# Rotary embedding in a decoder kernel: halves exchanged by transfers between partitions in place of a second projection, sine product on GpSimd

## The chip, the cores and the metric

The kernel runs on one core of a Trainium2 chip. The metric is the device time of one launch in microseconds (us). The matmul engine is TensorE (PE in the rows, with PEld for its weight loads), VectorE is DVE, ScalarE is ACT, GpSimd is POOL and SyncE, from whose queue the transfers are issued, is SP. All arithmetic is in float32.

## What is computed

A two-layer decoder over 8 batches of 512 rows of width 256. Each layer is self-attention, cross-attention and a feed-forward part, each added to its input and layer-normed. The change touches the self-attention of the second layer alone:

```python
q = einsum('bsd,qd->bsq', x, wq)            # 16 heads of 64
kv_latent = einsum('bsd,ld->bsl', x, w_kv_down)
k = einsum('bsl,ql->bsq', kv_latent, w_k_up)
v = einsum('bsl,ql->bsq', kv_latent, w_v_up)
q = q * cos + rotate_half(q) * sin          # rotate_half(x) = concat(-x[32:], x[:32]) in each head
k = k * cos + rotate_half(k) * sin
scores = q k^T / 8, causal; softmax; times v; times wo^T
```

## The kernel before

`decoder` runs its stages one after another: `attention("a0")`, a cross-attention, a butterfly FFN, `attention("a1")`, `attention("x1")` and a mixture of experts. Stage "a1" is the one in question. It handles 8 batches; a batch has G = 4 groups of 4 heads, a group has 4 tiles of 128 query rows, so a batch has 16 steps. Step s (0 to 15) is group s // 4, tile s % 4, and causality lets tile t see (t+1) x 128 keys.

The work is software-pipelined over steps. In step s PE forms the scores of tile s (`score_head`, L640), transposes the probabilities of tile s-3 (`transpose_head`, L668) and multiplies those of tile s-4 with the values (`times_values`, L689), ACT copies the transposed probabilities out of PSUM (L805) and takes the exponentials of tile s-1 (L810), DVE masks and maximises the scores (L993) and normalises tile s-2 (L1015). Each engine has its own instruction stream in the fixed order head j = 0, 1, 2, 3, then what is left at j = 4. Two heads' scores (j = 0, 1 and j = 2, 3) are made together.

`tasks` (L250) puts the rest between the heads. For the next group four *items* are made: for each of its two pairs of heads a q item (i even) and a k item (i odd). Items 0 and 1 stand in the group's first step, at j = 1 and j = 3, items 2 and 3 in its second. For the last group of a batch, the items belong to the next batch and stand one step later (steps 13 and 14), since step 12 holds the transposition of the next x ("xT") and the latent ("lat"). The values ("v", L596) come in the steps after, and the output projection of the previous batch ("y", L608), 16 matmuls each, stands at j = 1 of steps 4 to 7. A group's first scores wait until all low parts of its items are there (L622).

An item goes over four engines:

- PE (L537 to L547): the projection with the plain weights into one PSUM bank, then the one with weights whose halves of 32 columns are exchanged in each head (`wqs`, `wupk[:, 1]`) into the next. A q item has two contraction tiles, a k item one; the trace shows two matmul records for each.
- DVE (L939): plain times cos into `rsum[i % 2]`, exchanged times sin into `rsin`.
- POOL (L883): `rsum += rsin`; then (L887, L890) the low part, `rsum` less its high part.
- ACT (L751, L753): the high part. It doesn't stand at the item's own place but at the very end of the step (L824 to L827), item by item, and each waits for its `rot_sum`.

POOL's stream of an item is: wait for `rot_done`, add, wait for `hi` (the ACT copy), subtract. DVE starts an item only when the low part of the item two before it is there (L932). There are four PSUM banks `A` for scores and projections, taken in turn, and two, `T`, for the transposes: head j + 2 can be transposed when ACT has copied head j.

SP issues the stage's loads (L478, L480) and once per batch the next x tile (L486); otherwise it is idle here.

Of the kernel before, what the change touches and what calls it, by code (L numbers as in the profile page):

```python
# [212 lines left out]
def attention(nc, sh, kind, w):  # L213
# [68 lines left out]
    def work_jobs(work):  # L282
        if work[0] == "xT":
            return [(("xT", dt), "xt") for dt in range(DT)]
        if work[0] == "lat":
            return [("lat", "act")]
        if work[0] == "v":
            return [(work, "dve" if a0 else "v")]
        if work[0] == "y":
            return [(work, "dve")]  # L290
        if a1:
            return [((*work, 0), "dve"), ((*work, 1), "rot")]
        if x1:
            return [(work, "ql")]
        return [(work, ("dve", "kl")[work[2]])]
# [26 lines left out]
    with ExitStack() as ctx:  # L322
# [48 lines left out]
        if a1:  # L371
            wqs = sb("wqs", [P, DT, IN])
            lat = sb("lat", [P, S])
            wdn = sb("wdn", [P, DT, P])
            wupk = sb("wupk", [P, 2, IN])
            wupv = sb("wupv", [P, IN])
            cos = sb("cos", [P, S])
            sin = sb("sin", [P, S])
            rsum = sb("rsum", [P, 2, S])
            rsin = sb("rsin", [P, S])  # L380
# [41 lines left out]
        chain = sem("chain")  # L422
        sems = {"full": a_full, "act": a_act, "dve": a_dve, "xt": xt_done, "v": v_done,
# [43 lines left out]
        if a1:  # L467
            loads += [(wq[:], tiled(w["w_q"])), (wqs[:], tiled(w["w_q_swapped"])), (wdn[:], tiled(w["w_down"])),
                      (wupk[:, 0, :], w["w_up_k"]), (wupk[:, 1, :], w["w_up_k_swapped"]),
                      (wupv[:], w["w_up_v"]), (table[:], w["causal"]), (cos[:], w["cos"]), (sin[:], w["sin"])]  # L470
# [5 lines left out]
        @block.sync  # L476
        def _(sp):
            sp.dma_start(xin[:], sh.x_all[:, 0:QT, :]).then_inc(xin_in, 16)  # L478
            for to, src in loads:
                sp.dma_start(to, src).then_inc(weights, 16)  # L480
            if x1:
                sp.dma_start(ctxT[:], tiled(w["ctxT"][0])).then_inc(ctx_in, 16)
            with sp.Fori(1, B) as b:

                sp.wait_ge(xt_done, b * DT)
                sp.dma_start(xin[:], sh.x_all[:, bass.ds(b * QT, QT), :]).then_inc(xin_in, 16)  # L486
                if x1:

                    sp.wait_ge(v_done, b * N_V)
                    sp.dma_start(ctxT[:], w["ctxT"][bass.ds(b, 1)].rearrange("a (t p) n -> p (a t) n", p=P))\  # L490
                      .then_inc(ctx_in, 16)

        @block.tensor
        def _(pe):
# [13 lines left out]
            def project(seg, turn, b, work):  # L508
# [22 lines left out]
                if a1:  # L531
# [5 lines left out]
                    for sw in range(2):  # L537
                        name = (*work, sw)
                        pe.wait_ge(*seg.empty(turn, name))
                        bank = A[seg.bank(name)]  # L540
                        if i % 2 == 0:
                            for t in range(DT):
                                mm = pe.matmul(bank[:], (wq, wqs)[sw][:, t, col], xT[:, t, :],
                                               start=(t == 0), stop=(t == DT - 1))
                        else:
                            mm = pe.matmul(bank[:], wupk[:, sw, col], lat[:], start=True, stop=True)
                        mm.then_inc(a_full, 1)  # L547
# [189 lines left out]
        def _(act):  # L737
# [30 lines left out]

            def project(seg, turn, b, work):
# [18 lines left out]
            def step(seg, turn, b, s, prev, own, nxt):  # L788
# [8 lines left out]
                for j in range(5):  # L797
# [15 lines left out]
                    for at, work in found:  # L813
                        if at == j and not (a1 and work[0] == "item"):
                            project(seg, turn, b + (work in NEXT and s >= U - QT), work)
# [13 lines left out]
            def begin():  # L829
                for work in START:  # L830
                    project(start, 0, 0, work)
# [8 lines left out]
        def _(pool):  # L840
# [33 lines left out]
            if a1:  # L874
                pool.sem_inc(rot_sum, 2)
                pool.sem_inc(low, LOW_GROUP)
                pool.wait_ge(ready, N_READY)
                with pool.Fori(0, B) as b:
                    for g in range(G):
                        for i in range(4):  # L880
                            gp = g % 2
                            pool.wait_ge(rot_done, b * 4 * G + (4 * g + i + 1))
# [11 lines left out]
        def _(dve):  # L894
# [18 lines left out]
            def low_parts(seg, turn, b, g, i):  # L913
# [16 lines left out]
                elif a1:  # L930

                    dve.wait_ge(low, b * LOW_GROUP * G + (LOW_GROUP * g + (LOW_ITEM[i + 2] if i < 2 else LOW_GROUP + LOW_ITEM[i - 2])))  # L932
                    for sw in range(2):
                        name = ("item", g, i, sw)
                        if sw:

                            dve.wait_ge(rot_sum, b * 4 * G + (4 * g + i + 2))
                        dve.wait_ge(*seg.full(turn, name))
                        nc.vector.tensor_tensor((rsum[:, i % 2, :], rsin[:])[sw], A[seg.bank(name)][:], (cos, sin)[sw][:],  # L939
                                                ALU.mult).then_inc((a_dve, rot_done)[sw], 1)  # L940
# [1148 lines left out]
def combine(nc, sh, place, gates, results, out):  # L2089

    with ExitStack() as ctx:  # L2091
# [58 lines left out]
        "a1_w_q", "a1_w_q_swapped", "a1_w_down", "a1_w_up_k", "a1_w_up_k_swapped", "a1_w_up_v", "a1_w_o",  # L2150
# [44 lines left out]
def laid_out(a):  # L2195
# [6 lines left out]
    def swapped(wt):  # L2202

        n = wt.shape[0]
        return wt.reshape(n, -1, 2, 32)[:, :, ::-1].reshape(n, -1)

# [21 lines left out]
    def placed_high(wt, side):  # L2228

        out = np.zeros((HIGH, FT, P, 2), np.float32)  # L2230
        for h in range(HIGH):
# [19 lines left out]
            "a1_w_q": wq1, "a1_w_q_swapped": swapped(wq1), "a1_w_down": a["L1_attn_w_kv_down"].T,  # L2251
            "a1_w_up_k": wku1, "a1_w_up_k_swapped": swapped(wku1), "a1_w_up_v": a["L1_attn_w_v_up"].T,
# [24 lines left out]
```

## Time and profile before

| | us |
|---|---|
| median of 3 runs (lowest, highest) | 4617.55 (4616.95, 4618.64) |
| the profiled execution: its own time | 4615.9 |
| its span, first to last instruction | 4614.1 |
| PE, DVE, ACT, POOL busy in the span | 3915.6, 2717.7, 2094.8, 1178.2 |
| mean granted TensorE clock | 0.932 |

The page's list by line gives busy time and what ended the idle time before. Matmuls are pipelined, so the pace of a run of matmuls is read from the start of one group of records to the start of the next, not from one record's length. Times of a timeline are from the start of the span. Stage "a1" lies between 1562 us (its first load) and 2779 us.

### The profile page before, as it was taken

To read this page: it belongs to the slowest core of one execution; us is meant where nothing else is said; L and a number is where in the kernel's file an instruction comes from. 1 tells how busy PE (TensorE), PEld (TensorE's weight loads), DVE (VectorE), ACT (ScalarE), POOL (GpSimd) and SP (SyncE) were. 2 spreads that over 40 slices of the span, in tenths; PEclk is the share of its full clock that TensorE was granted. 3 is DMA by queue.
4 is the path that set the end of the run, shared out by engine and by line. 5 is a ranking of instruction groups with operands and counts; after the bars stand their busy time and mean duration, and the time that the engine had idled before them with its cause. 6 is when DMAs were issued, how large, how long until landed. Compare 5 with 4: busy or idle time off the path is not lost. (4 is left out here: it accounts for less than half of the span.)

```text
span 4614.1 us, 81513 instructions
## 1 busy us (share of the span) xinstructions
PE 3915.6 (85%) x25804; PEld 2614.9 (57%) x25805; DVE 2717.7 (59%) x7518; ACT 2094.8 (45%) x4994; POOL 1178.2 (26%) x980
## 2 busy tenths in 40 slices
PE   6999999996869799999999997999999526999980
PEld 3555555565768555555555565666666414666650
DVE  5888888886867466666665654566656421111116
ACT  4777776772342165455545553555555201111110
POOL 2444444443400132232222211122111251000004
PEclk9999999997789899999999998999999758999995
DMA  2000000001020100000000001000000521000003
GB/s 64 6 6 6 6 6 6 1 1 46 14 85 1 59 6 6 1 6 6 6 1 6 1 1 44 7 6 5 5 6 1 172 105 47 30 30 30 30 30 106
DMA packets 80047, 115.62 MB, mean 25 GB/s; under 512 B 14369, under 2 KB 66017, under 8 KB 78945
## 3 DMA queue, kind: packets, MB, share of 16 engines
q1 hardware_dynamic: 73568, 94.56, 6.1%
q0 software_dynamic: 6144, 16.79, 1.2%
q8 instruction: 187, 3.06, 0.3%
q14 instruction: 148, 1.20, 0.1%
HBM read 63.09 MB, written 31.46 MB: 20 GB/s over the span
## 5 line engine op out<-in xcount | busy, mean ns | idle before, releaser
L805 ACT ACTIVATE a_pT<-a_T 128x512 f32<-128x512 f32 (+3 forms) x1024 | 526.0, 514 | 469.8 <-PE a_T L668 460.2
L810 ACT ACTIVATE a_t<-a_t,a_neg 128x512 f32<-128x512 f32 (+3 forms) x1024 | 650.7, 635 | 97.8 <-DVE a_neg L1007 97.4
L668 PE MATMUL a_T<-ident,a_t 128*128 128x128 f32 x3328 | 554.1, 283 | 6.5 <-ACT a_pT L805 6.2
L1015 DVE TENSOR_SCALAR a_t<-a_t,a_inv 128x512 f32<-128x512 f32 (+3 forms) x768 | 528.0, 688 | 9.0
L668 PEld LDWEIGHTS a_T<-ident,a_t 128*128 128x128 f32 x3328 | 396.6, 142 | 171.1 <-issue 68.4
L629 PE MATMUL a_A<-a_kpad,a_qs 128*128 128x512 f32 x1024 | 393.5, 467 | 72.0 <-DVE a_mx L993 50.8
L883 POOL TENSOR_TENSOR a_rsum<-a_rsum,a_rsin 128x512 f32<-128x512 f32 x128 | 162.7, 1271 | 978.0 <-DVE a_rsin L939 976.9
L854 POOL TENSOR_TENSOR a_t<-a_t,a_inv 128x512 f32<-128x512 f32 x256 | 284.2, 1132 | 477.3 <-DVE a_inv L1011 477.3
L993 DVE CUSTOM_DVE_ANT_0 a_t<-a_A,a_decay 128x512 f32<-128x512 f32 x512 | 343.9, 683 | 85.9 <-PE a_A L629 62.2
L993 DVE CUSTOM_DVE_ANT_0 a_t<-a_A,a_table 128x384 f32<-128x384 f32 (+3 forms) x512 | 247.2, 483 | 171.1 <-PE a_A L640 166.9
L854 POOL TENSOR_TENSOR x_t<-x_t,x_inv 128x576 f32<-128x576 f32 x128 | 158.1, 1257 | 725.0 <-DVE x_inv L1011 725.0
L2072 DVE COPY experts_y<-experts_Y 128x256 f32<-128x256 f32 x72 | 30.6, 425 | 514.0 <-PE experts_Y L2010 514.0
L2022 PE MATMUL experts_H<-ex_w,experts_xgT 128*128 x576 | 268.2, 609 | 47.6 <-ACT experts_xgT L2049 47.6
L629 PEld LDWEIGHTS a_A<-a_kpad,a_qs 128*128 128x128 f32 x1024 | 161.7, 193 | 210.1 <-issue 108.7
L805 ACT ACTIVATE x_pT<-x_T 128x512 f32<-128x512 f32 (+1 forms) x320 | 189.3, 592 | 177.8 <-PE x_T L668 135.7
L2010 PE MATMUL experts_Y<-ex_w,experts_hT 128*128 x1152 | 260.5, 379 | 1.0 <-DVE experts_hT L2081 1.0
L2010 PEld LDWEIGHTS experts_Y<-ex_w,experts_hT 128*128 128x128 f32 x1152 | 218.8, 190 | 61.3 <-issue 35.2
L2113 POOL DMA_INDIRECT combine_got<-moe_results,moe_place x64 | 60.9, 951 | 691.5 <-PEq L2091 658.0
L993 DVE CUSTOM_DVE_ANT_0 x_t<-x_A,x_table 128x512 f32<-128x512 f32 x256 | 170.9, 685 | 107.2 <-PE x_A L640 105.1
L689 PE MATMUL a_O<-a_pT,a_v 128*64 128x128 f32 x2560 | 210.9, 286 | 25.0 <-ACT a_oT L822 23.7
L685 PE MATMUL a_O<-a_pT,a_v 128*32 128x128 f32 x4096 | 221.5, 290 | 3.9 <-ACT a_pT L805 3.9
L640 PE MATMUL a_A<-a_khl,a_qhl 64*128 64x128 f32 (+3 forms) x1536 | 188.0, 350 | 38.5 <-issue 15.4
(275 smaller groups left out, 7387.8 us busy)
## 6 DMA issues: line engine op xcount, KB each, us to landing
ex_w<-in_f_w_dram SPq DMA_DIRECT2D x16, 1024.0 KB, 13.6
moe_sent<-route_zeros SPq DMA_DIRECT2D x1, 9216.0 KB, 29.6
experts_xg<-moe_sent SPq DMA_DIRECT2D x72, 128.0 KB, 2.0
moe_results<-experts_y SPq DMA_DIRECT2D x72, 128.0 KB, 1.7
a_xin<-x_all SPq DMA_DIRECT2D x16, 512.0 KB, 2.9
x_xin<-x_all SPq DMA_DIRECT2D x16, 512.0 KB, 2.9
x_all<-in_x_dram SPq DMA_DIRECT2D x1, 4096.0 KB, 14.5
out_dram<-x_all SPq DMA_DIRECT2D x8, 512.0 KB
```

The source lines that it names most:

```text
L629: mm = pe.matmul(A[seg.bank(name)][:, 0:keys(u)], qs[:, gp, q], kpad[:, gp, hl, j, 0:keys(u)], start=(n == 0), stop=(n == 1))
L640: mm = pe.matmul(A[seg.bank(at)][:, 0:keys(u)], q_hl[r, gp, ql, j // 2, q], k_hl[r, gp, kl_, j // 2, 0:keys(u)], start=(n == 0), stop=(n = ...
L668: mm = pe.transpose(bank[:, kt, :], t_of(u, j, kt * P, (kt + 1) * P), sh.ident[:])
L685: mm = pe.matmul(O[hh][32 * j:32 * j + 32, q], v_sb[:, kt, 8 * hh + 2 * j + par, :], p_tile(u, j, kt), start=(par == 0 and qt == 0 and kt ...
L689: mm = pe.matmul(O[pr][64 * half:64 * half + 64, q], v_sb[:, kt, col], p_tile(u, j, kt), start=(kt == 0), stop=last, skip_group_check=True)
L805: nc.scalar.activation(to, of, ACT.Copy).then_inc(t_empty, 1)
L810: nc.scalar.activation(t_of(u_e % U, j, 0, n), t_of(u_e % U, j, 0, n), ACT.Exp, bias=neg[:, slot, j:j + 1], scale=SCALE, accum_out=total[: ...
L854: nc.gpsimd.tensor_tensor(t_of(u_n % U, j, 0, NK), t_of(u_n % U, j, 0, NK), inv[:, u_n % 4, j:j + 1].to_broadcast([P, NK]), ALU.mult).then ...
L993: nc.vector.tensor_tensor_reduce(t_of(s, j, 0, n), A[seg.bank(name)][:, 0:n], table[:, at:at + n], 1.0, LOWEST, ALU.mult if a0 else ALU.ad ...
L1015: nc.vector.tensor_scalar(t_of(u_n % U, j, 0, m), t_of(u_n % U, j, 0, m), inv[:, u_n % 4, j:j + 1], None, ALU.mult).then_inc(normed, 1)
L2010: mm = pe.matmul(Y[parity][:], hT[:, f, :], w2[:, bass.ds(e, 1), f, :].rearrange("p a d -> p (a d)"), start=(f == 0), stop=(f == FT - 1))
L2022: mm = pe.matmul(H[half][:], xgT[:, dt, :], w1[:, bass.ds(e, 1), dt, half * 512:(half + 1) * 512] .rearrange("p a f -> p (a f)"), start=(d ...
```

## The change

The exchanged projections and their weights go. ACT copies each item's raw projection from PSUM to `raw` (four buffers) at the item's own place in the step; SP issues four transfers, each of 32 partitions x 2 KB, that write it to `raw_swapped` (two buffers) with neighbouring blocks of 32 partitions exchanged; POOL multiplies that with sin into `rsin` and then adds and subtracts as before. DVE keeps the cos product. Its wait for the raw copy is new, and the bank is now counted free by the cos product. The high part stays on ACT at the end of the step.

```diff
-            return [((*work, 0), "dve"), ((*work, 1), "rot")]
+            return [(work, "rot")]
...
-            wqs = sb("wqs", [P, DT, IN])
-            wupk = sb("wupk", [P, 2, IN])
+            wupk = sb("wupk", [P, IN])
+            raw = sb("raw", [P, 4, S])
+            raw_swapped = sb("rawswapped", [P, 2, S])
...
+            def swap_halves(b, n):
+
+                wait_apart(sp, (weights, 16 * len(loads)), (raw_done, b * 4 * G + n + 1), (sin_done, b * 4 * G + n + 3))
+                for k in range(4):
+                    sp.dma_start(raw_swapped[32 * k:32 * k + 32, n % 2, :],
+                                 raw[32 * (k ^ 1):32 * (k ^ 1) + 32, n % 4, :]).then_inc(swapped[n % 2], 16)
+
+            if a1:
+                with sp.Fori(0, B - 1) as b:
+                    for n in range(4 * G):
+                        swap_halves(b, n)
+                        if n == 3:
+                            sp.wait_ge(xt_done, b * DT + DT)
+                            sp.dma_start(xin[:], sh.x_all[:, bass.ds(b * QT + QT, QT), :]).then_inc(xin_in, 16)
...
-                    for sw in range(2):
-                        name = (*work, sw)
-                        pe.wait_ge(*seg.empty(turn, name))
-                        bank = A[seg.bank(name)]
...
+                    pe.wait_ge(*seg.empty(turn, work))
+                    bank = A[seg.bank(work)]
+                    if i % 2 == 0:
+                        for t in range(DT):
+                            mm = pe.matmul(bank[:], wq[:, t, col], xT[:, t, :], start=(t == 0), stop=(t == DT - 1))
+                    else:
+                        mm = pe.matmul(bank[:], wupk[:, col], lat[:], start=True, stop=True)
+                    mm.then_inc(a_full, 1)
...
+            def raw_copy(seg, turn, b, work):
+                _, g, i = work
+                n = 4 * g + i
+                act.wait_ge(*seg.full(turn, work))
+                act.wait_ge(sin_done, b * 4 * G + n + 1)
+                nc.scalar.activation(raw[:, n % 4, :], A[seg.bank(work)][:], ACT.Copy).then_inc(raw_done, 1)
...
-                        if at == j and not (a1 and work[0] == "item"):
-                            project(seg, turn, b + (work in NEXT and s >= U - QT), work)
+                        if at == j:
+                            (raw_copy if a1 and work[0] == "item" else project)(
+                                seg, turn, b + (work in NEXT and s >= U - QT), work)
...
                 for work in START:
+                    if a1 and work[0] == "item":
+                        raw_copy(start, 0, 0, work)
                     project(start, 0, 0, work)
...
+                pool.sem_inc(sin_done, 4)
...
-                            pool.wait_ge(rot_done, b * 4 * G + (4 * g + i + 1))
+                            n = 4 * g + i
+                            pool.wait_ge(swapped[n % 2], b * 32 * 4 * G + 64 * (n // 2 + 1))
+                            nc.gpsimd.tensor_tensor(rsin[:], raw_swapped[:, n % 2, :], sin[:],
+                                                    ALU.mult).then_inc(sin_done, 1)
+                            pool.wait_ge(sin_done, b * 4 * G + (n + 5))
+                            pool.wait_ge(rot_done, b * 4 * G + (n + 1))
                             nc.gpsimd.tensor_tensor(rsum[:, i % 2, :], rsum[:, i % 2, :], rsin[:],
                                                     ALU.add).then_inc(rot_sum, 1)
                             pool.wait_ge(hi, b * HI_GROUP * G + (HI_GROUP * g + HI_ITEM[i]))
...
-                    for sw in range(2):
-                        name = ("item", g, i, sw)
-                        if sw:
-
-                            dve.wait_ge(rot_sum, b * 4 * G + (4 * g + i + 2))
-                        dve.wait_ge(*seg.full(turn, name))
-                        nc.vector.tensor_tensor((rsum[:, i % 2, :], rsin[:])[sw], A[seg.bank(name)][:], (cos, sin)[sw][:],
-                                                ALU.mult).then_inc((a_dve, rot_done)[sw], 1)
+                    name = ("item", g, i)
+                    dve.wait_ge(*seg.full(turn, name))
+                    dve.wait_ge(raw_done, b * 4 * G + (4 * g + i + 1))
+                    nc.vector.tensor_tensor(rsum[:, i % 2, :], A[seg.bank(name)][:], cos[:], ALU.mult)\
+                      .then_inc(rot_done, 1)
```

## Rows read from the trace of the kernel before

**Rows 1.** Busy time by stretch: us, busy (instructions) of each engine, PEclk, DMA, GB/s.

```profile
1724.00:2620.00 896.00, 839.64 (x5268) 508.17 (x5266) 560.86 (x1704) 468.20 (x1365) 246.92 (x192) 0.99 0.01 4
```

**Rows 2.** Timeline of PE, first scores of groups 0 to 3, step 13, next batch.

```profile
2023.22 0.55 PE L640 MATMUL a_A<-a_khl,a_qhl 64*128 64x128 f32 x6 [2.98 <-issue]
...
2055.21 0.55 PE L640 MATMUL a_A<-a_khl,a_qhl 64*128 64x128 f32 x6
...
2100.46 0.55 PE L640 MATMUL a_A<-a_khl,a_qhl 64*128 64x128 f32 x6
...
2134.25 0.55 PE L640 MATMUL a_A<-a_khl,a_qhl 64*128 64x128 f32 x6
...
2142.20 0.62 PE L640 MATMUL a_A<-a_khl,a_qhl 64*128 64x256 f32 x6
...
2172.62 0.55 PE L640 MATMUL a_A<-a_khl,a_qhl 64*128 64x128 f32 x6 [2.92 <-issue]
```

**Rows 3.** Timeline of PE: step 1's items of group 0, and where step 3 begins.

```profile
2037.39 1.88 PE L543 MATMUL a_A<-a_xT,a_wqs 128*128 128x512 f32 x4
2039.20 0.62 PE L640 MATMUL a_A<-a_khl,a_qhl 64*128 64x256 f32 x6
...
2040.47 1.88 PE L546 MATMUL a_A<-a_lat,a_wupk 128*128 128x512 f32 x4
2042.28 0.79 PE L640 MATMUL a_A<-a_khl,a_qhl 64*128 64x384 f32 x6
...
2048.97 0.96 PE L640 MATMUL a_A<-a_khl,a_qhl 64*128 64x512 f32 x6
```

**Rows 4.** Timeline of ACT at the turn of steps 0 and 1.

```profile
2036.25 0.63 ACT L753 ACTIVATE a_khl<-a_rsum 128x512 fp32r<-128x512 f32 x1 [2.61 <-POOL a_rsum L883]
2036.79 0.47 ACT L805 ACTIVATE a_pT<-a_T 128x384 f32<-128x384 f32 x1
...
2037.54 0.48 ACT L805 ACTIVATE a_pT<-a_T 128x384 f32<-128x384 f32 x1
```

**Rows 5.** Timeline of POOL, and one operation of DVE, over the same steps.

```profile
2034.94 1.27 POOL L883 TENSOR_TENSOR a_rsum<-a_rsum,a_rsin 128x512 f32<-128x512 f32 x1
2036.96 1.41 POOL L890 TENSOR_TENSOR a_khl<-a_rsum,a_khl 128x512 fp32r<-128x512 f32 x1 [0.74 <-ACT a_khl L753]
...
2031.02 1.45 DVE L1015 TENSOR_SCALAR a_t<-a_t,a_inv 128x384 f32<-128x384 f32 x1
```

**Rows 6.** Transfers: issues with KB each and us to landing; one line's issue ns.

```profile
a_xin<-x_all SPq DMA_DIRECT2D x16, 512.0 KB, 2.9
x_ctxT<-in_ctxT_dram SPq DMA_DIRECT2D x8, 64.0 KB, 1.9
moe_results<-experts_y SPq DMA_DIRECT2D x72, 128.0 KB, 1.7
L490 SPq DMA_DIRECT2D x_ctxT<-in_ctxT_dram x7: 376/381/406, 2847.3 to 3452.7; - x7
```

**Rows 7.** Timeline of PE: the last batch's first item, and an output projection.

```profile
2619.50 0.55 PE L640 MATMUL a_A<-a_khl,a_qhl 64*128 64x128 f32 x6
...
2622.19 1.88 PE L543 MATMUL a_A<-a_xT,a_wq 128*128 128x512 f32 x4
...
1758.84 3.62 PE L608 MATMUL a_A<-a_wo,a_oT 128*128 128x256 f32 x16
```

**Rows 8.** Busy time by stretch after PE's idle time at a batch's end.

```profile
2024.00:2027.60 3.60, 3.60 (x15) 1.96 (x14) 1.26 (x7) 2.17 (x6) 0.00 (x0) 0.55 0.02 5
2028.00:2029.00 1.00, 1.00 (x4) 0.43 (x3) 0.51 (x1) 0.00 (x0) 0.00 (x0) 1.00 0.00 0
```

**Rows 9.** Timeline of the stage's start: PE's first work, second projection, first scores.

```profile
1580.49 1.94 PE L517 MATMUL a_A<-ident,a_xin 128*128 128x128 f32 x8 [26.38 <-DVEq L911]
...
1588.80 1.88 PE L543 MATMUL a_A<-a_xT,a_wqs 128*128 128x512 f32 x4
...
1604.58 0.90 PE L640 MATMUL a_A<-a_khl,a_qhl 64*128 64x128 f32 x6 [5.31 <-POOL a_khl L890]
```

More of the change, by code:

```diff
@@ L422, in attention @@
         chain = sem("chain")
+        raw_done = env.sem("raw_done") if a1 else None
+        swapped = [env.sem(f"swapped{i}") for i in range(2)] if a1 else None
+        sin_done = env.sem("sin_done") if a1 else None
         sems = {"full": a_full, "act": a_act, "dve": a_dve, "xt": xt_done, "v": v_done,
@@ L467, in attention @@
         if a1:
-            loads += [(wq[:], tiled(w["w_q"])), (wqs[:], tiled(w["w_q_swapped"])), (wdn[:], tiled(w["w_down"])),
-                      (wupk[:, 0, :], w["w_up_k"]), (wupk[:, 1, :], w["w_up_k_swapped"]),
+            loads += [(wq[:], tiled(w["w_q"])), (wdn[:], tiled(w["w_down"])),
+                      (wupk[:], w["w_up_k"]),
                       (wupv[:], w["w_up_v"]), (table[:], w["causal"]), (cos[:], w["cos"]), (sin[:], w["sin"])]
@@ L482, in _ @@
                 sp.dma_start(ctxT[:], tiled(w["ctxT"][0])).then_inc(ctx_in, 16)
+            def swap_halves(b, n):
[10 more added lines that the diff above has]
+                            sp.dma_start(xin[:], sh.x_all[:, bass.ds(b * QT + QT, QT), :]).then_inc(xin_in, 16)
+                for n in range(4 * G):
+                    swap_halves(B - 1, n)
+                return
             with sp.Fori(1, B) as b:
@@ L536, in project @@
                         pe.wait_ge(a_act, b + 1)
-                    for sw in range(2):
-                        name = (*work, sw)
-                        pe.wait_ge(*seg.empty(turn, name))
-                        bank = A[seg.bank(name)]
[L541 to L547, printed above, removed]
+                    pe.wait_ge(*seg.empty(turn, work))
[6 more added lines that the diff above has]
+                    mm.then_inc(a_full, 1)
                     return
@@ L2149 @@
         "f0_w_exp_b", "f0_low", "f0_high", "f0_up_bias", "f0_w_con", "f0_b_con", "f0_down_bias",
-        "a1_w_q", "a1_w_q_swapped", "a1_w_down", "a1_w_up_k", "a1_w_up_k_swapped", "a1_w_up_v", "a1_w_o",
+        "a1_w_q", "a1_w_down", "a1_w_up_k", "a1_w_up_v", "a1_w_o",
         "x1_w_q", "x1_w_k1", "x1_w_v1", "x1_w_k2", "x1_w_v2", "x1_w_o", "x1_b_o",
@@ L2200, in split_pairs @@
         return wt.reshape(n, 2, 4, 2, 16).transpose(0, 1, 3, 2, 4).reshape(n, 4, 64)
-    def swapped(wt):
-        n = wt.shape[0]
-        return wt.reshape(n, -1, 2, 32)[:, :, ::-1].reshape(n, -1)
     def pairs(stage):
@@ L2250, in laid_out @@
             "f0_down_bias": a["L0_ffn_down_bias"].reshape(row),
-            "a1_w_q": wq1, "a1_w_q_swapped": swapped(wq1), "a1_w_down": a["L1_attn_w_kv_down"].T,
-            "a1_w_up_k": wku1, "a1_w_up_k_swapped": swapped(wku1), "a1_w_up_v": a["L1_attn_w_v_up"].T,
+            "a1_w_q": wq1, "a1_w_down": a["L1_attn_w_kv_down"].T,
+            "a1_w_up_k": wku1, "a1_w_up_v": a["L1_attn_w_v_up"].T,
             "a1_w_o": a["L1_attn_wo"].T,
```

## Prediction

> **What bounds the kernel now.** The change lies inside stage "a1", so I read the busy times of that stage by stretch first, then the order of PE's work through one batch, then ACT and POOL beside it, as the change lengthens a chain that runs over these two. In the six steady batches PE is busy for 839.6 of 896 us, at a granted clock of 0.99 of 2.4 GHz, ACT for 468, DVE for 561, POOL for 247 [rows 1]. PE sets the pace; its only long idle time is 3 us at each batch's end. One batch takes 149.4 us: its groups 32.0, 45.2, 33.8 and 38.4 us, the last with 8.0 for step 12 [rows 2]. Group 1 carries four output projections of 3.6 us [rows 7].
>
> The place to look at is the end of a step with items. ACT takes the first item's high part, then idles 2.6 us until the second item's sum is there [rows 4]: POOL subtracts (1.28 us) and adds (1.27 us) in between [rows 5]. That idle time costs PE nothing today, since PE has projections to run meanwhile.
>
> **What goes.** Per q item four matmul records on exchanged weights, 2037.39 to 2039.20 with 0.1 for the next operation: 1.72 us. Per k item two of the four in 2040.47 to 2042.28: 0.86 us [rows 3]. 64 items of each kind: 64 x 2.58 = 165 us, 5.2 us per group, all on the engine that sets the pace. Were nothing else to happen, this would be the gain, 3.6%. DVE loses 128 products, worth nothing by themselves, as it is busy 63% of the stage [rows 1]. Two of the stage's loads go, 1.5 of 5.5 MB; PE starts 18 us after the stage's first load [rows 9], and a quarter of the bytes is 4 us (bounds 0 and 5).
>
> **What comes, priced from R, the end of an item's raw copy on ACT.** SP wakes (0.1 us, the gap ACT to POOL in [rows 4, 5]), issues four transfers of 64 KB; an issue is 0.38 us, so I take 0.4 from one to the next and the fourth starts 1.3 us after R; landing 1.9 us after issue [rows 6]. Landed at R + 3.3. No row shows a 32-partition transfer inside SBUF: the nearest are 64 KB (1.9), 128 KB (1.7) and, inside SBUF but 512 KB, 2.9. I take the one of equal size; bounds for the landing R + 2.7 and R + 4.6. Then POOL's product, an operation of the add's form, 1.27 + 0.05, the add 1.27 + 0.05, ACT's high part with wake 0.7: R + 6.6. POOL's subtraction, 1.35: R + 7.95. Only now comes the second item's product in POOL's stream, 1.25, its add, 1.3, and ACT's second high part, 0.7: **ACT is free at R + 11.2 us**. The second item's transfers are hidden behind the first's, its POOL work isn't.
>
> The raw copies are on ACT, priced like the high part's, 0.6 us [rows 4], 128 x 0.6 = 77 us; they lie partly in time in which ACT waits. SP's 512 issues block nothing but the next x tile, which is needed ten steps later. One more POOL operation per item also collides with DVE: a normalisation took 1.45 us beside POOL's add [rows 5]. DVE's slack covers that; if all of an operation's 1.27 us were waited for, without cover, it would be 163 us in all.
>
> What queues behind ACT's two waits: its copies of transposed probabilities. PE can go on through the next step's first scores, heads 0 and 1, and an item, up to the transpose of head 2, which needs a T bank that only ACT empties. The slack there is 5.0 us after the last item of the step (scores 0.55, two transposes and two value products 2.1, item 1.8, scores 0.55, [rows 3]). R is 1.2 us before that last item's end (scores and two transposes 1.0, the k item 0.9, less the 0.7 of the copy), so PE stands from about R + 6.2 until R + 11.8. DVE's new wait for the raw copy comes through the same ACT stall; as the cos product is all that hangs on it, and POOL needs that only after its own product, I cost it at nothing; if that cover went, it would be up to 0.7 us in a step.
>
> **The cycle of a group** (F: ACT free).
> - First scores to R of item 0: 2.7 to the projection's start, 1.8 projection, 0.6 copy: 5.1 [rows 7]; 5.8 at a batch's start, with the low clock there.
> - R to the R of item 2: 11.2 to F, two heads' copy and exponential at 0.75, copy 0.6: 13.3. In group 3, where the exponentials are 256 keys wide in place of 128, I estimate 0.95 for a head: 13.7.
> - R of item 2 to F: 11.2.
> - F to the next group: transpose 0.55 later, then 0.5, value product 0.6, transpose 0.5, values 1.0, 3.3 with the waits, and step 3 from [rows 3, 2]: 2048.97 to 2055.21, 6.2. Sum 9.5. In group 3 it is step 15's rest, 4.1 with two value blocks, and 3.0 idle at the loop's end: 7.1.
> - Clock: after the 3 us idle at a batch's end the granted clock was 0.55 for 3.6 us, the lower of its two levels for nearly all of it [rows 8], so 1.6 us of work are lost. The second stall's aftermath is such a place; the first one's lies under the second. 1.6 per group.
>
> So group 0: 5.8 + 13.3 + 11.2 + 9.5 + 1.6 = 41.4 (was 32.0). Group 2: 40.7 (was 33.8). Group 1: two of its four output projections (step 5's and 6's) fall into stalls, two don't: 40.7 + 7.2 = 47.9 (was 45.2). Group 3: 8.0 + 5.1 + 13.7 + 11.2 + 7.1 + 1.6 = 46.7 (was 38.4). A batch grows by 9.4 + 6.9 + 2.7 + 8.3 = 27.3 us, six of them 164. The last batch has no items in group 3: 19. The first has no output projections: I take 10 for group 0, whose before is shortest, and 24 for the others: 34. At the start the four items go strictly one after another, 6.6 + 0.6 each, from R at 1589.5 (the first projection ends where the exchanged one begins, 1588.8, and the copy takes 0.7): low parts at 1619 in place of 1604.6 [rows 9]: 14. Loads -4. **Sum: +227 us.** On the profiled execution's 4615.9 us that is 4843; the median of the runs lies 1.7 us above it, so 4845, 4.9% slower.
>
> A rule that would make it another way: the Trainium skill, "DMA: Bandwidth & Descriptors", Rules for kernel authors, says to issue a transfer early, compute, and wait late, so that its fixed cost overlaps. By it the sum would be -165 - 4; the order of POOL's stream, with the product first and ACT waiting for it in the same step, is why I don't take it.
>
> **Rivals.**
> 1. *The chain is covered* (faster). If PE isn't held at the transpose of head 2 because the two waits on ACT end within its slack, R + 6.2, only the removal counts: 4617.6 - 169 = 4449 us. For it: today's 2.6 us of ACT idle costs nothing, ACT is idle for 48% of the stage [rows 1]. Against: POOL's five operations and two ACT copies alone, with no transfer at all, are 7.9 us after R. It decides from a chain of R + 6.2 us down; even a landing at once leaves it longer. Between, each us off the chain is worth some 66 us (two chains per group, 62, and the start's four). Break-even needs 3.4 us off, a landing with R. Chance 0.05.
> 2. *The clock stays low* (much slower). With two idle spells per 20 us, PE could stay at 1.2 GHz through the 14.6 us between F and the next R, which is PE's own time: up to 13 us more for 31 groups, 5250 us. Against: after that idle time the clock is full again four microseconds later [rows 8]. Chance 0.05.
> 3. *Less slack lost than counted*: ACT makes up for its stall faster, and the output projections and norm steps hide more of it; half of the added time, 4730 us. For it: group 2's own 1.8 us over group 0 today are waits that a stalled ACT would hide. Chance 0.10.
> 4. That the exchanged matmuls stay is excluded by the diff; no chance.
>
> **The numbers.** The forecast has 0.80. Bounds within it: the chain's landing from 2.7 to 4.6 makes -40 and +86; the clock term 0 to twice its size -50 and +50; they rarely add up. Range 4725 to 4945, so that it takes in rival 3. About 0.2% (9 us) is what a measurement of this kernel can tell from no change: faster by more 0.06, within 0.01, slower by more 0.93.
>
> **What would show it.** Right: ACT idle before L751 as well as before L753, about 3.5 and 4 us each time, ended by POOL's add; POOL idle before its product, ended by a transfer or the raw copy; PE idle before L668, ended by ACT's copy L805, some 5 us twice per group; PE busy in the stage 165 us less plus what the clock costs; groups of 41, 48, 41 and 47 us. Wrong: PE's wait for L805 stays under 1 us (rival 1), a mean granted clock near 0.5 in the stage (rival 2), or landings far from 1.9 us. If the transfers were late beyond R + 4.6, POOL's idle time before the product would exceed 3 us of each pair and the sum would be too small.

## The result, and the profile after

The changed kernel takes 4908.9 us (median of four runs, 4905.6 to 4919.4) against 4617.6 for the kernel before in the same comparison: a ratio of **1.063**, 95% interval 1.0616 to 1.0653. That is +291 us; forecast were +227 and 4845, with a range up to 4945. The profiled execution took 4911.5 us, its span is 4909.6.

First the page of the kernel after: its head, three groups of its part 5 (busy us, mean ns of one | idle us of the engine just before them and what ended it) and one line of part 6 (KB each, us from issue to landing).

```profile
span 4909.6 us, 81900 instructions
PE 3877.1 (79%) x25420; PEld 2615.2 (53%) x25421; DVE 2647.1 (54%) x7390; ACT 2168.4 (44%) x5122; POOL 1337.5 (27%) x1108
L686 PE MATMUL a_T<-ident,a_t 128*128 128x128 f32 x3328 | 599.3, 300 | 321.6 <-ACT a_pT L830 321.3
L913 POOL TENSOR_TENSOR a_rsin<-a_rawswapped,a_sin 128x512 f32<-128x512 f32 x128 | 162.8, 1272 | 1122.3 <-DMA a_rawswapped<-a_raw 1122.3
L970 DVE TENSOR_TENSOR a_rsum<-a_A,a_cos 128x512 f32<-128x512 f32 x128 | 88.6, 692 | 371.6 <-ACT a_raw L792 370.5
a_rawswapped<-a_raw SPq DMA_DIRECT2D x512, 64.0 KB, 2.0
```

PE now idles 321.6 us before its transposes, for ACT's copy that empties the T bank. In the kernel before, the same group stands with 6.5 us. Yet PE's busy time fell by 38.5 us only (3915.6 before), though the removed matmuls are worth 165. The stage alone says why; first the kernel before, then the kernel after, each from the stage's first load to the next stage's, to within 0.3 us (busy times of PE, PEld, DVE, ACT, POOL, then the granted clock). The kernel before ends this stage at 2786 us, not at 2779: its last layer norm runs until 2785.7.

```profile
1562.00:2786.00 1224.00, 1118.91 (x7008) 677.97 (x7008) 743.37 (x2272) 624.21 (x1817) 328.63 (x256) 0.98 0.03 9
```

```profile
1567.45:3075.14 1507.69, 1075.24 (x6624) 675.43 (x6624) 672.97 (x2145) 698.44 (x1945) 488.29 (x384) 0.85 0.11 29
2006.00:2008.00 2.00, 2.00 (x14) 1.34 (x13) 0.00 (x0) 1.72 (x6) 0.15 (x1) 0.50 0.03 8
```

The stage grew by 284 us. PE's busy time there fell by 44, so, if the removed records were worth the forecast's 165 us, those that stayed are 165 - 44 = 121 us longer, at a clock of 0.85 in place of 0.98. PE's idle time grew from 105 to 432 us, by 327. And -165 + 121 + 327 is these 284 us, but for rounding. The lower row is a stretch just after a stall: PE works all the time, at 0.50, the lower of its two levels.

The third view is the timeline of PE, at the first scores of batch 0, of batch 1, and of one later batch's four groups and the next batch (start us, length us).

```profile
1624.16 0.69 PE L658 MATMUL a_A<-a_khl,a_qhl 64*128 64x128 f32 x4 [21.23 <-POOL a_khl L924]
1792.22 0.55 PE L658 MATMUL a_A<-a_khl,a_qhl 64*128 64x128 f32 x6
...
1973.25 0.44 PE L658 MATMUL a_A<-a_khl,a_qhl 64*128 64x128 f32 x4 [0.32 <-issue]
2016.09 0.44 PE L658 MATMUL a_A<-a_khl,a_qhl 64*128 64x128 f32 x4
2066.66 0.44 PE L658 MATMUL a_A<-a_khl,a_qhl 64*128 64x128 f32 x4
2108.72 0.44 PE L658 MATMUL a_A<-a_khl,a_qhl 64*128 64x128 f32 x4
2155.62 0.54 PE L658 MATMUL a_A<-a_khl,a_qhl 64*128 64x128 f32 x5 [1.31 <-ACT a_v L809]
...
2883.75 0.55 PE L658 MATMUL a_A<-a_khl,a_qhl 64*128 64x128 f32 x6
```

The groups take 42.8, 50.6, 42.1 and 46.9 us (forecast 41.4, 47.9, 40.7, 46.7; [rows 2] has before). Batch 0 takes 168.1 us, the six steady ones 1091.5, or 181.9 each where 149.4 were [rows 1, 2].

Last the chain itself, in the timeline of all engines in group 3 of that batch; the answer to [rows 4, 5].

```profile
2121.50 0.60 ACT L792 ACTIVATE a_raw<-a_A 128x512 f32<-128x512 f32 x1 [1.74 <-PE a_A L562]
2122.18 5.03 SPq L491 DMA_DIRECT2D a_rawswapped<-a_raw  x8
...
2126.11 1.27 POOL L913 TENSOR_TENSOR a_rsin<-a_rawswapped,a_sin 128x512 f32<-128x512 f32 x1 [26.89 <-DMA a_rawswapped<-a_raw]
2127.54 1.26 POOL L917 TENSOR_TENSOR a_rsum<-a_rsum,a_rsin 128x512 f32<-128x512 f32 x1 [0.16 <-POOL a_rsin L913]
2128.83 0.63 ACT L769 ACTIVATE a_qhl<-a_rsum 128x512 fp32r<-128x512 f32 x1 [4.30 <-POOL a_rsum L917]
...
2130.76 1.26 POOL L913 TENSOR_TENSOR a_rsin<-a_rawswapped,a_sin 128x512 f32<-128x512 f32 x1
...
2133.47 0.63 ACT L771 ACTIVATE a_khl<-a_rsum 128x512 fp32r<-128x512 f32 x1 [4.01 <-POOL a_rsum L917]
2134.01 0.58 ACT L830 ACTIVATE a_pT<-a_T 128x512 f32<-128x512 f32 x1
2134.73 1.08 PE L686 MATMUL a_T<-ident,a_t 128*128 128x128 f32 x4 [5.46 <-ACT a_pT L830]
```

R, the end of the raw copy, is 2122.10. POOL's product starts at R + 4.0, the second high part ends at R + 12.0, and 0.6 us later PE starts the transpose for which it has waited 5.46 us.

### The profile page after: what moved, and what is told of

It reads as the page before. It is cut to its first block and busy times, and to the rows that moved or that the text cites. A ratio compares the mean times of both kernels' runs of the same rounds, so it can differ in the third digit from the quotient of the medians.

```text
span 4909.6 us, 81900 instructions
## 1 busy us (share of the span) xinstructions
PE 3877.1 (79%) x25420; PEld 2615.2 (53%) x25421; DVE 2647.1 (54%) x7390; ACT 2168.4 (44%) x5122; POOL 1337.5 (27%) x1108
## 5 line engine op out<-in xcount | busy, mean ns | idle before, releaser
L686 PE MATMUL a_T<-ident,a_t 128*128 128x128 f32 x3328 | 599.3, 300 | 321.6 <-ACT a_pT L830 321.3
L686 PEld LDWEIGHTS a_T<-ident,a_t 128*128 128x128 f32 x3328 | 423.4, 151 | 508.7 <-issue 400.0
L913 POOL TENSOR_TENSOR a_rsin<-a_rawswapped,a_sin 128x512 f32<-128x512 f32 x128 | 162.8, 1272 | 1122.3 <-DMA a_rawswapped<-a_raw 1122.3
L647 PE MATMUL a_A<-a_kpad,a_qs 128*128 128x512 f32 x1024 | 394.7, 469 | 72.3 <-DVE a_mx L1024 47.7
L970 DVE TENSOR_TENSOR a_rsum<-a_A,a_cos 128x512 f32<-128x512 f32 x128 | 88.6, 692 | 371.6 <-ACT a_raw L792 370.5
L707 PE MATMUL a_O<-a_pT,a_v 128*64 128x128 f32 x2560 | 229.8, 304 | 31.5 <-ACT a_oT L848 25.8
L658 PE MATMUL a_A<-a_khl,a_qhl 64*128 64x128 f32 (+3 forms) x1536 | 205.1, 376 | 50.2 <-POOL a_khl L924 21.2
L658 PEld LDWEIGHTS a_A<-a_khl,a_qhl 64*128 64x128 f32 x1536 | 126.4, 203 | 213.5 <-issue 112.4
```

Source lines behind the costliest of these rows:

```text
L647: mm = pe.matmul(A[seg.bank(name)][:, 0:keys(u)], qs[:, gp, q], kpad[:, gp, hl, j, 0:keys(u)], start=(n == 0), stop=(n == 1))
L658: mm = pe.matmul(A[seg.bank(at)][:, 0:keys(u)], q_hl[r, gp, ql, j // 2, q], k_hl[r, gp, kl_, j // 2, 0:keys(u)], start=(n == 0), stop=(n = ...
L686: mm = pe.transpose(bank[:, kt, :], t_of(u, j, kt * P, (kt + 1) * P), sh.ident[:])
L707: mm = pe.matmul(O[pr][64 * half:64 * half + 64, q], v_sb[:, kt, col], p_tile(u, j, kt), start=(kt == 0), stop=last, skip_group_check=True)
L913: nc.gpsimd.tensor_tensor(rsin[:], raw_swapped[:, n % 2, :], sin[:], ALU.mult).then_inc(sin_done, 1)
```

## The experiments

**Theory A** is the forecast's: each pair of items is a serial chain over ACT, SP, the transfer and POOL; its two waits stand in ACT's fixed order ahead of the copies that empty the T banks, so PE stands. The price is 66 us of time per us of chain. **Theory B**: the time is the extra product on GpSimd itself, its collisions with DVE and the lower clock; the wait is a symptom. Ratios are to the kernel before on the same chip, with their 95% intervals.

### The chain shortened and lengthened

*No transfer.* POOL reads the raw copy directly, and SP's transfers go: the kernel leaves out the exchange of halves.

```diff
-                            pool.wait_ge(swapped[n % 2], ...)
-                            nc.gpsimd.tensor_tensor(rsin[:], raw_swapped[:, n % 2, :], sin[:],
+                            pool.wait_ge(raw_done, b * 4 * G + (n + 1))
+                            nc.gpsimd.tensor_tensor(rsin[:], raw[:, n % 4, :], sin[:],
```

> Edit: SP issues no exchange; POOL multiplies the raw copy itself with sin, so the rotation takes the wrong halves (the exchange is left out). Theory A (the chain from an item's raw copy R to ACT's release sets PE's pace; two such chains per group with items, 62, and four items at the start, so 66 us of time per us of chain): POOL starts 0.1 us after R in place of 4.0, the chain falls from 12.0 to 8.1 us, 3.9 x 66 = 257 us less: 4652 us (4600 to 4700). Theory B (the transfers are covered by the rest of ACT's and POOL's order; the loss is the POOL product and PE's lower clock): at most 60 us less, 4850 or more.

4630.9 us, 1.0065 (1.0048 to 1.0082), within theory A's bounds and far below theory B's 4850. PE's idle time before the transposes is 95 us instead of 322:

```profile
L669 PE MATMUL a_T<-ident,a_t 128*128 128x128 f32 x3328 | 576.2, 291 | 95.1 <-ACT a_pT L813 94.0
```

*Doubled.* Four more transfers per item, into a buffer that nobody reads, ahead of the four that count; POOL waits for all eight.

```diff
-                for k in range(4):
-                    sp.dma_start(raw_swapped[...
+                for k, to in [(k, to) for to in (twin, raw_swapped) for k in range(4)]:
+                    sp.dma_start(to[...
```

> Edit: four more transfers of the same size, to a buffer that nobody reads, issued ahead of the four that count. Theory A: 4 x 0.6 us of issue more on the chain, 2.4 x 66 = 158 us: 5067 us (5030 to 5110), and ACT's wait before L769 2.4 us longer, the one before L771 unchanged. Theory B: below 4950.

5093.9 us, 1.1075 (1.1057 to 1.1094). The chain in its timeline:

```profile
2214.49 0.59 ACT L793 ACTIVATE a_raw<-a_A 128x512 f32<-128x512 f32 x1
...
2217.60 2.49 SPq L492 DMA_DIRECT2D a_rawswapped<-a_raw  x4
...
2221.59 1.26 POOL L914 TENSOR_TENSOR a_rsin<-a_rawswapped,a_sin 128x512 f32<-128x512 f32 x1 [7.60 <-DMA a_rawswapped<-a_raw]
...
2226.82 1.26 POOL L914 TENSOR_TENSOR a_rsin<-a_rawswapped,a_sin 128x512 f32<-128x512 f32 x1 [0.54 <-DMA a_rawswapped<-a_raw]
...
2229.53 0.63 ACT L772 ACTIVATE a_khl<-a_rsum 128x512 fp32r<-128x512 f32 x1 [4.59 <-POOL a_rsum L918]
```

From R (2215.08) to ACT free (2230.16) it is 15.1 us, 3.1 more than after: 2.5 for the first item, and 0.54 because SP's sixteen issues now make the second item's landing late too. The expectation had 2.4 for the first and nothing for the second, so it was short: the time rose by 206 us against the changed kernel (by the ratios, below), where 158 were expected.

*POOL's order.* Both products and sums of a pair first, then both subtractions; `rsin` has two buffers.

```diff
-                        for i in range(4):
...
+                        for pair in range(2):
+                            for i in (2 * pair, 2 * pair + 1):
...
+                                nc.gpsimd.tensor_tensor(rsum[:, i % 2, :], rsum[:, i % 2, :], rsin[:, i % 2, :],
+                                                        ALU.add).then_inc(rot_sum, 1)
+                            for i in (2 * pair, 2 * pair + 1):
...
+                                nc.gpsimd.tensor_tensor(part[:, gp, 1, i // 2, :], rsum[:, i % 2, :],
+                                                        part[:, gp, 0, i // 2, :], ALU.subtract).then_inc(low, 1)
```

> Edit: POOL does product and sum of both items of a step before it waits for the first high part; rsin gets a second buffer. Theory A: the second sum is ready at R + 4.0 + 4 x 1.35 = R + 9.4 in place of R + 11.4, ACT is free at R + 10.1, 1.9 us earlier, in 62 chains (not at the start): 4909 - 118 = 4791 us (4760 to 4830). Theory B, in which POOL's number of operations or its collisions with DVE count: no change, since POOL does the same operations.

4769.7 us, 1.0371 (1.0354 to 1.0389). POOL does the same operations as in the changed kernel, so by theory B nothing should have changed. In its timeline the second product no longer waits behind the first item's subtraction:

```profile
1987.97 0.60 ACT L792 ACTIVATE a_raw<-a_A 128x512 f32<-128x512 f32 x1 [4.09 <-PE a_A L562]
...
1992.54 1.27 POOL L914 TENSOR_TENSOR a_rsin<-a_rawswapped,a_sin 128x512 f32<-128x512 f32 x1 [23.23 <-DMA a_rawswapped<-a_raw]
...
1995.35 1.28 POOL L914 TENSOR_TENSOR a_rsin<-a_rawswapped,a_sin 128x512 f32<-128x512 f32 x1
...
1998.00 0.63 ACT L771 ACTIVATE a_khl<-a_rsum 128x512 fp32r<-128x512 f32 x1 [2.12 <-POOL a_rsum L918]
```

R to ACT free is 10.1 us, 1.9 less than after.

The changed kernel itself, run once more on a second chip, gives the fixed point (4907.4 us, 1.0621, 1.0605 to 1.0638):

> The changed kernel itself, once more, as the yardstick of this chip, on which the kernel before takes 4601 us in place of 4617. Both theories: the same ratio as on record, 1.063 (1.061 to 1.066), 4893 us.

From the mean of its two ratios, 1.0628, the steps are -2.6% of 4601 us for 1.9 us less chain (118 us, 62 per us), +4.5% for 3.1 us more (206 us, 66 per us) and -5.6% for the 3.9 us between R and the start of POOL's product (259 us, 66 per us). The stage alone, from its first load to the next stage's, is free of what chips and runs differ by elsewhere: it takes 1507.7 us in the changed kernel, 1382.5 with POOL's new order, 1710.7 doubled and 1249.0 with no transfer, so 66, 65.5 and 66 us per us. Three points on one line: the slope that the prediction set.

### One part at a time

*The sine product on DVE*, at the end of DVE's step, with the transfers kept.

```diff
+            def sine(b, g, i):
...
+                nc.vector.tensor_tensor(rsin[:], raw_swapped[:, n % 2, :], sin[:], ALU.mult).then_inc(sin_done, 1)
...
-                            nc.gpsimd.tensor_tensor(rsin[:], raw_swapped[:, n % 2, :], sin[:],
-                                                    ALU.mult).then_inc(sin_done, 1)
```

> Edit: the transfers stay, the sine product goes back to DVE, which makes it at the end of the step from the exchanged copy in SBUF. Theory A: the chain loses POOL's two products but for one of DVE's: R + 4.0, product 0.8, sum 1.35, high part 0.7, subtraction 1.35, sum 1.3, high part 0.7: ACT free at R + 10.2 in place of R + 12.0, 1.8 x 66 = 119 us less, ratio to before about 1.037. Theory B (DVE, standing until the second item's transfer has landed, becomes what PE waits for): not below 1.055.

4809.9 us, 1.0414 (1.0399 to 1.0430).

```profile
L992 DVE TENSOR_TENSOR a_rsin<-a_rawswapped,a_sin 128x512 f32<-128x512 f32 x128 | 99.3, 776 | 168.5 <-DMA a_rawswapped<-a_raw 163.9 <-POOL a_rsum L914 4.3
L686 PE MATMUL a_T<-ident,a_t 128*128 128x128 f32 x3328 | 591.7, 297 | 186.3 <-ACT a_pT L830 168.4 <-DVE a_t L1049 17.6
L658 PE MATMUL a_A<-a_khl,a_qhl 64*128 64x128 f32 (+3 forms) x1536 | 201.1, 369 | 93.7 <-DVE a_mx L1027 63.7
```

The product is shorter there (776 ns in place of 1272) and off POOL, which takes 99 us off the change, where 119 were expected. For DVE's order now holds the wait for the transfer, and PE waits for DVE as well: 17.6 us before the transposes, and 63.7 before scores, where the changed kernel has 10.2.

*The second projection back*, read by ACT's raw copy and POOL's product; no transfers. It asks what the copy and the product cost by themselves.

```diff
-            return [(work, "rot")]
+            return [((*work, 0), "rot"), ((*work, 1), "raw")]
...
+                                mm = pe.matmul(bank[:], (wq, wqs)[sw][:, t, col], xT[:, t, :],
...
-                nc.scalar.activation(raw[:, n % 4, :], A[seg.bank(work)][:], ACT.Copy).then_inc(raw_done, 1)
+                nc.scalar.activation(raw[:, n % 4, :], A[seg.bank((*work, 1))][:], ACT.Copy).then_inc(raw_done, 1)
```

> Edit: the transfers are undone and the second projection is back; ACT copies the exchanged projection from PSUM and POOL multiplies that with sin. What is left of the change is the product on GpSimd and ACT's copy. Theory A: the chain is that of the kernel without transfer, R + 8.1, and PE's 165 us come back but fill the holes in which PE stands there (94 us before L668): 4631 + 165 - 94 less some 30 us of low clock = 4672 us, ratio 1.015 (1.005 to 1.025). Theory B (the product's place on GpSimd is the main loss): above 1.04.

4736.7 us, 1.0258 (1.0242 to 1.0274): just above what was expected.

```profile
L673 PE MATMUL a_T<-ident,a_t 128*128 128x128 f32 x3328 | 570.4, 289 | 65.5 <-ACT a_pT L817 64.6
L551 PE MATMUL a_A<-a_lat,a_wupk 128*128 128x512 f32 x256 | 126.6, 617 | 18.5 <-DVE a_rsum L956 15.4 <-ACT a_raw L779 3.1
```

PE's new waits are 59 us for ACT and some 11 for a bank; the mean clock falls from 0.93 to 0.92. So the change can be taken apart: product and copy, with the matmuls kept, +119 us (this run); the matmuls' removal brings -89 of the 165 (from here to the kernel with no transfer, 1.0258 to 1.0065); the transfers add 259. Together +289, as these are steps along one row of ratios. Of the 165 a part is lost again in waits: PE's wait for ACT before the transposes rises from 64.6 to 94.0 us, that for DVE before these scores from 14.4 to 44.8. And the prices hold for this order of steps: with the waits put later (below), the same transfers cost 43 us, not 259.

### The wait put later

*Deferred.* ACT takes the high parts one step later, at j = 2 and 4, so that the chain has a whole step; POOL's order as above, four buffers of `rsum`, and at the stage's start all four raw copies come ahead of the first high part.

```diff
+                late = [(at, work) for at, work in tasks(s - 1, prev, own, nxt) if work[0] == "item"] \
+                    if a1 and own and s > 0 else []
...
+                    for at, work in late:
+                        if at + 1 == j:
+                            project(seg, turn, b + (work in NEXT and s - 1 >= U - QT), work)
...
-                for _, work in found:
-                    if a1 and work[0] == "item":
-                        project(seg, turn, b + (work in NEXT and s >= U - QT), work)
```

> Edit: as pool_order, and ACT takes an item's high part one step later (at j = 2 and j = 4 of the next step), with four rsum buffers, so that ACT and PE don't wait inside the step in which the item was made. Theory A: PE isn't held; the 165 us of exchanged projections are won, less some waits in the batch's last step: 4490 us (4440 to 4560), PE's wait for ACT's copies under 50 us in the stage, clock back at 0.98 or more. Theory B (clock, collisions of POOL with DVE, or ACT's extra copies): above 4750.

4532.8 us, 0.9844 (0.9823 to 0.9865): **faster than both kernels**. Transfers, product on GpSimd and raw copies are all there as in the changed kernel; only the order of POOL's and ACT's streams differs, and some 360 us are gone: 118 with POOL's order (1.0371 above), the rest with the later waits, of which 12.5 at the stage's start (first scores 44.2 us after its first load in place of 56.7). That decides against theory B as the main cause; what it names comes back below, in a smaller size. Placed one head earlier still (j = 1 and 3), it is the same, 4545.6 us on the second chip, 0.9842 (0.9829 to 0.9856):

```diff
-                        if at + 1 == j:
+                        if at == j:
```

> Edit: as deferred, with each high part one head earlier (j = 1 and j = 3 of the next step). Theory A: each batch's end, where PE waited 4.0 us for the last low part and then ran at the low clock, comes 1 to 2 us earlier; against that ACT may wait up to 1 us for the first sum (ready at R + 6.7, when the next step's j = 1 comes). Between 20 us less and 10 us more than deferred: ratio to before 0.980 to 0.987. Theory B, that PE is held by ACT again at this place: above 0.99.

But it is some 55 us short of what theory A expected (4490 us where the kernel before takes 4617, a ratio of 0.972; the removed matmuls alone would be 0.964), and the clock in the stage is 0.93, not back at 0.98. In the stage PE idles 165 us in place of 105, and the records that stayed are some 31 us longer. The list by line of the deferred kernel:

```profile
L686 PE MATMUL a_T<-ident,a_t 128*128 128x128 f32 x3328 | 564.8, 287 | 2.3 <-ACT a_pT L832 1.8
L658 PE MATMUL a_A<-a_khl,a_qhl 64*128 64x128 f32 (+3 forms) x1536 | 196.7, 363 | 107.6 <-POOL a_khl L926 47.7 <-DVE a_mx L1026 46.2 <-ACT a_xT L799 9.9
```

The stall at the transposes is gone, and 94 us stand before scores instead: 47.7 for the last low part before a batch's first scores, 46.2 for a maximum of DVE (5.3 and 7.0 in the kernel before). The latter in its timeline, in group 2:

```profile
2079.32 1.27 POOL L917 TENSOR_TENSOR a_rsin<-a_rawswapped,a_sin 128x512 f32<-128x512 f32 x1 [16.01 <-DMA a_rawswapped<-a_raw]
...
2083.63 1.22 DVE L173 SCALAR_TENSOR_TENSOR a_scratch<-a_scratch 128x4 f32<-128x4 f32 x1
2084.80 1.26 POOL L926 TENSOR_TENSOR a_qhl<-a_rsum,a_qhl 128x512 fp32r<-128x512 f32 x1
2084.96 4.11 DVE L145 TENSOR_SCALAR x_all<-x_all,a_mv,a_scratch  x4
...
2087.29 1.31 POOL L917 TENSOR_TENSOR a_rsin<-a_rawswapped,a_sin 128x512 f32<-128x512 f32 x1
2089.59 0.41 DVE L1026 CUSTOM_DVE_ANT_0 a_t<-a_A,a_table 128x256 f32<-128x256 f32 x1
...
2090.06 1.33 PE L658 MATMUL a_A<-a_khl,a_qhl 64*128 64x384 f32 x6 [6.10 <-DVE a_mx L1026]
```

POOL runs almost without a gap from 2079 to 2089, and beside it DVE's layer norm stretches: four operations of L145 take 4.11 us, the one of L173 on 128 x 4 elements 1.22. At their own lengths (0.41 and 0.16, below) they would be 3.5 us shorter, over half of the 6.10 that PE waits; what the rest is isn't shown. Two more runs ask what belongs to which.

*The kernel before, deferred in the same way*: its second projection stays, no transfers.

```diff
-                            dve.wait_ge(rot_sum, b * 4 * G + (4 * g + i + 2))
+                            dve.wait_ge(rot_sum, b * 4 * G + (4 * g + i + 1))
...
+                    for at, work in late:
+                        if at + 1 == j:
+                            project(seg, turn, b + (work in NEXT and s - 1 >= U - QT), work)
```

> The kernel before, with its second projection and without transfers, but with the reordering of the deferred kernel: ACT's high parts one step later, POOL's two sums of a pair ahead of its two subtractions, four buffers of rsum and two of rsin. It asks how much of the deferred kernel's 0.984 is the reordering and how much the removed matmuls. Theory A (PE's own work sets the pace of before, its ACT idle time of 2.6 us costs nothing): the reordering gives nothing there, 4610 to 4625 us on a chip where before takes 4617, a ratio of 0.998 to 1.005 (the low parts of each batch's last items come some 4 us later, which may cost up to 30 us, 1.006). Rival C (the held ACT already cost something before): 0.985 to 0.995, and then the exchange by transfers would bring little of its own.

4584.2 us, 0.9968 (0.9956 to 0.9981): the reordering brings 0.3% by itself, between theory A's best case (0.998, at the interval's edge) and rival C's least (0.995, outside it), so that the held ACT cost at most a little in the kernel before. So of the deferred kernel's 1.6%, some 1.2% (0.9844 / 0.9968 = 0.988) belong to the exchange by transfers.

*Deferred, no transfer*, edited as in the first experiment:

```diff
-                                nc.gpsimd.tensor_tensor(rsin[:, i % 2, :], raw_swapped[:, n % 2, :], sin[:],
+                                nc.gpsimd.tensor_tensor(rsin[:, i % 2, :], raw[:, n % 4, :], sin[:],
```

> The deferred kernel with no transfers: POOL multiplies the raw projection itself with sin, so the exchange of halves is left out. It asks where the deferred kernel loses the 1.9% that lie between its 0.984 and the 0.965 of the removed matmuls alone. Theory A: the transfers are hidden but for one place, the last low part of each batch's items, for which PE waits 4.0 us eight times; without the landing of 4.0 us that wait goes, with the low clock after it: 30 to 50 us less than the deferred kernel, a ratio to before of 0.973 to 0.978. Rival D (the loss is the collision of DVE and POOL, and ACT's 128 raw copies, all of which stay): within 10 us of the deferred kernel, 0.982 to 0.987.

4484.6 us, 0.9750 (0.9734 to 0.9766), 43 us below the deferred kernel by the ratios. The size is theory A's, the place only in part. For the kernel before deferred, then for the deferred one without transfers, the scores in the list by line:

```profile
L640 PE MATMUL a_A<-a_khl,a_qhl 64*128 64x128 f32 (+3 forms) x1536 | 187.6, 349 | 35.3 <-POOL a_khl L890 21.9 <-ACT a_xT L774 9.9 <-DVE a_mx L993 3.1
```

```profile
L641 PE MATMUL a_A<-a_khl,a_qhl 64*128 64x128 f32 (+3 forms) x1536 | 190.0, 353 | 81.7 <-POOL a_khl L909 37.1 <-DVE a_mx L1009 33.0 <-ACT a_xT L782 9.9
```

The wait for the low part fell only from 47.7 to 37.1, and nearly half of that at the stage's start (15.5 to 10.8); the wait for DVE fell from 46.2 to 33.0, and the kernel's mean clock rose from 0.917 to 0.927. So the expectation named the place wrongly: the 43 us are spread over both waits and the clock after them. The layer norm of the stage, between 1600 and 2750 us, in the kernel before deferred, the deferred one, and the one without transfers (length of one in ns: least, median, most):

```profile
L145 DVE TENSOR_SCALAR x_all<-x_all,a_mv,a_scratch x28: 406/407/414, 1820.0 to 2701.4; - x24, 128x256 f32<-128x256 f32 x4
```

```profile
L145 DVE TENSOR_SCALAR x_all<-x_all,a_mv,a_scratch x32: 400/1345/1382, 1808.7 to 2715.3; - x24, 128x256 f32<-128x256 f32 x8
```

```profile
L145 DVE TENSOR_SCALAR x_all<-x_all,a_mv,a_scratch x32: 399/407/1411, 1797.4 to 2666.5; - x24, 128x256 f32<-128x256 f32 x8
```

The same operation takes 0.41 us, or 1.35 to 1.41 where POOL works beside it; without transfers it meets POOL less often. What stays without transfers comes with the product on GpSimd or with the raw copies on ACT, which no deferred run parts: 33 us of waiting for DVE where the kernel before, deferred, has 3.

## Why the prediction was right, and where it was short

Sign and mechanism held, and the runs back them. By its own steps:

- **The matmuls' 165 us** went, 384 records fewer in the stage (7008 and 6624 are counted, as in the forecast's four and two per item). It was right not to take them as a gain against the chain: without transfers only 89 of them came through.
- **The chain.** Forecast R + 11.2, measured R + 12.0 in the pair shown and 12.1 at the mean of the 62 pairs in groups. The step that failed is "an issue is 0.38 us, so I take 0.4 from one to the next": SP's issues of these transfers take 0.59 us at the median, and the first landing is at R + 4.0, not 3.3. The landing itself, 2.0 against 1.9, was right. 0.16 more is POOL's wait for its own product. (POOL's 1.28 us for a subtraction is the median of that line; the operation in [rows 5] took 1.41. This moved nothing.) In group 1 of each steady batch the first chain is longer still, 12.4 to 13.4 us, with a late landing (R + 5.5 in one of them); why is open. 0.9 us in each of 62 chains is 56 us; the batches are off by 52 (below).
- **PE's idle time before the transposes**: 5.2 us for each of 62 stalls (321.6), forecast 5.6; ACT before L769 and L771, 4.2 and 4.1 us each, forecast 3.5 and 4. The step from ACT's hold to PE's stall is right to 7%.
- **The clock.** Forecast 1.6 us per group, 50 in all; the rows show PE's remaining records 121 us longer in the stage. These 71 us more don't lengthen the stage by as much. Where the forecast put its 1.6, between the second chain's end and the next group's first scores, the six steady batches took 11.6 us in group 0 and 11.9 in group 2, forecast 11.1. By elimination, most other longer records lie ahead of the stalls, where ACT's chain sets the time and not PE.
- **Errors that cancel.** In the six steady batches the chains are 42 us over the forecast and all else is 11 under: the batch's end took 6.6 us, forecast 8.7, and group 1 outside its chains 24.3, forecast 25.5, against 0.4 and 0.8 more in groups 0 and 2. That the groups fit to 1.4, 2.7, 1.4 and 0.2 us is in part luck.
- **The ends.** The start cost 13.9 us (1624.16 less 1604.58 [rows 9], less the 5.7 by which the stage began later), forecast 14 - 4. The lighter loads brought their 4: PE's first work comes 15.0 us after the stage's first load, before 18.7. But the four items in a row took 32.5 us from R to the first scores, forecast 29.5, by the same late landing. Batch 0 grew by 48, forecast 34; the six steady ones by 197, forecast 164; the last by 25, forecast 19.
- **Outside the stage**, priced at nothing, are 12 us: 5.7 ahead of it and 6.6 behind. No line of that code changed, and the traces say that it needn't be the change: over all twelve profiled runs stage "a1" begins between 1561.4 and 1567.7 us, and what lies behind it takes 1827.7 to 1839.0 us in the four runs on the chip of the changed kernel's second run, and 1810.0 to 1815.9 in the six on two other chips. What makes these differences is open.

Sum: 4 + 14 + 33 + 6 + 12 is, unrounded, 68.5 us, the difference between 295.5 (the spans) and 227.

Rival 1 (covered) is out: even with no transfer at all PE waits 95 us, as its "against" had said. Rival 2 (clock low throughout) is out: 0.85 in the stage. Rival 3 (half) is out. The range needed its upper half, and would have been too low for a landing beyond R + 4.6.

The rule that the prediction weighed, the Trainium skill, "DMA: Bandwidth & Descriptors", Rules for kernel authors (issue early, compute, wait late), speaks of what the changed kernel does not do: the deferred one waits late, and goes from 1.037, with POOL's order alone, to 0.984. The trace agrees with it in sign; of the -169 us that it would have given, -72 came, for the waits shown above and the clock after them.

## What to carry to other kernels

When a cheaper path is longer in time, look for the engine whose fixed order holds its wait, and for what is queued behind that wait; here 1 us of chain cost 66 us, and POOL's order with two waits moved by one step turned +6% into -1.6%. Order the operations of a shared engine by who waits for them (both sums ahead of both subtractions: 118 us). Test a transfer by itself in three ways: away, doubled, and waited for later. Its price is that of its wait: 259 us for these transfers with the wait in the same step, 43 with the wait one step later.

## What was not expected of the hardware

- These transfers of 32 partitions x 2 KB inside SBUF issue slower than the line of equal size from HBM in [rows 6] (0.38 us): 0.51 to 1.77 us, median 0.59, over all 512 (SP's instructions, lengths in ns). That the place is the reason isn't shown: the kernel before issues this stage's larger loads from HBM in 0.43 to 1.08 us each.

```profile
L491 SPq DMA_DIRECT2D a_rawswapped<-a_raw x512: 507/591/1767, 1591.7 to 2998.9; - x171
```

- An operation of DVE beside one of POOL can take several times its own length, small ones most: in the deferred kernel 128 x 4 elements (L167, L173) took up to 1.22 and 1.23 us there and 0.16 alone, 128 x 256 (L145) 1.35 and 0.41. The forecast had taken 1.45 for a normalisation beside the add and called DVE's slack cover enough; it is in the changed kernel, but not in the deferred one. The Trainium skill, "SBUF — State Buffer", Who interferes with whom, has a rule for it: the two share a pair of ports, a DVE instruction wants it when it runs in a 2-port mode or has two inputs in SBUF, and the loser is blocked for the whole instruction of the other. The trace agrees: what is added, 1.07 and 0.94 us, is near one POOL operation's 1.27, whatever the size of DVE's own.
- A stall of 5 to 6 us costs again afterwards, in the clock: PE's transposes take 300 ns at the mean over the changed kernel, 283 over the kernel before, 287 once the wait is moved, in the order of PE's idle time in the stage (432, 105 and 165 us).
